# Third stage of a three-stage attention kernel: both runs of value products placed between head outputs and scores in TensorE's order

## The reference, cut to what matters

```python
def attn_layer(x, Wqkv, qs, ksc, Wo):                 # 16 heads of 64
    q, k, v = split(x @ Wqkv)                         # per head
    q = rotary(l2norm(q) * qs); k = rotary(l2norm(k) * ksc)
    sim = where(mask, -max, (q @ k.T) * 8.0)
    return (softmax(sim) @ v) @ Wo
for i in range(6):
    x = attn_layer(shift_tokens(x), ...) + x
    x = ffn_layer(shift_tokens(x), ...) + x           # layer norm, W1, a * gelu(gate), W2
```

## Time and profile before

| what | value |
|---|---|
| time, median of 3 runs | 3528.43 us (3526.76 to 3532.59) |
| time of the profiled execution | 3525.89 us |
| its span (first to last instruction) | 3524.1 us |
| TensorE busy | 3377.9 us, 96% of the span |
| VectorE / ScalarE / GpSimd busy | 2811.5 / 2792.7 / 2475.5 us |
| mean granted TensorE clock | 0.993 of full speed |

### The profile page before, as it was taken

The page is one execution under the profiler, slowest core; times in us unless marked ns, Lnnn a source line. Parts: engine busy times, 40 slices in busy tenths (PEclk is TensorE's granted clock), DMA queues, the critical chain, the costliest instruction groups (busy, mean ns, idle before and its releaser), DMA issues.

```text
span 3524.1 us, 120975 instructions
## 1 busy us (share of the span) xinstructions
PE 3377.9 (96%) x49605; PEld 2495.3 (71%) x49605; DVE 2811.5 (80%) x5297; ACT 2792.7 (79%) x5522; POOL 2475.5 (70%) x4812
## 2 busy tenths in 40 slices
PE   8989997999999999999999999999999999999997
PEld 5778774677777777777777777777777777777776
DVE  6834445888888888888888888888888888888885
ACT  5756664688888888888888888888888888888885
POOL 5622224777777777777777777777777777777774
PEclk9999998999999999999999999999999999999999
DMA  3000002444444444444444444444444444444441
GB/s 101 3 10 8 9 6 50 92 82 82 82 81 89 95 82 82 80 88 97 82 82 82 83 90 93 82 82 80 90 96 83 82 82 88 78 85 83 88 85 39
DMA packets 200382, 260.17 MB, mean 74 GB/s; under 512 B 123161, under 2 KB 145438, under 8 KB 199838
## 3 DMA queue, kind: packets, MB, share of 16 engines
q0 software_dynamic: 55296, 201.35, 30.4%
q1 hardware_dynamic: 143820, 50.88, 5.8%
q10 hardware_dynamic: 722, 0.21, 0.0%
HBM read 23.95 MB, written 2.10 MB: 7 GB/s over the span
## 4 chain that ended last, share of the span: by engine, by line
PE 78%; issue 2%; DVE 1%; POOL 1%; DMA 1%; ACT 0%; SPq 0%; POOLq 0%; DVEq 0%
PE bank L1032 18%; PE bank L1008 16%; PE bank L1083 10%; PE bank L1160 10%; PE bank L1128 7%; PE bank L1144 6%; PE bank L1103 5%; PE bank L1024 3%; PE bank L1098 2%; DVE R L1319 1%; DMA R<-R 1%; POOL R L1432 0%; POOL P L1444 0%; DVE ss L1332 0%; POOL P L1438 0%
## 5 line engine op out<-in xcount | busy, mean ns | idle before, releaser
L1319 DVE TENSOR_TENSOR R<-bank,tables 128x1024 f32<-128x1024 f32 x768 | 903.6, 1218 | 167.5 <-ACT sq L1219 127.4
L1032 PE MATMUL bank<-WA,xcT 128*128 128x512 f32 x1536 | 757.6, 596 | 1.8 <-ACT xcT L1194 1.8
L1008 PEld LDWEIGHTS bank<-ident,R 128*128 128x128 f32 x3072 | 371.6, 141 | 307.0 <-issue 299.9
L1444 POOL TENSOR_TENSOR P<-P,inv_sum 128x512 f32<-128x512 f32 x384 | 458.2, 1193 | 13.1 <-DVE inv_sum L1373 12.1
L1332 DVE TENSOR_REDUCE ss<-sq 128x16 f32<-128x1024 f32 x384 | 460.3, 1199 | 0.0
L1219 ACT ACTIVATE sq<-bank 128x512 f32<-128x512 f32 x768 | 438.2, 595 | 23.9 <-PE bank L1032 23.5
L1432 POOL TENSOR_TENSOR R<-R,rn 128x512 f32<-128x512 f32 x384 | 392.3, 1042 | 88.1 <-DMA R<-R 73.4
L1008 PE MATMUL bank<-ident,R 128*128 128x128 f32 x3072 | 429.8, 273 | 3.3 <-POOL R L1432 2.4
L1438 POOL TENSOR_TENSOR P<-P,rn 128x512 f32<-128x512 f32 x384 | 402.5, 1048 | 2.1 <-DVE P L1361 2.1
L1160 PE MATMUL bank<-WO,OT 128*128 128x128 f32 x3072 | 386.4, 279 | 1.7 <-ACT OT L1194 1.7
L1083 PE MATMUL bank<-WV,xcT 128*64 128x512 f32 x1536 | 376.0, 606 | 3.2 <-DVE R L1319 2.9
(11 more groups left out here) (154 smaller groups left out, 7082.5 us busy)
## 6 DMA issues: line engine op xcount, KB each, us to landing
R<-R POOLq DMA_DIRECT2D x384, 512.0 KB, 5.3
WA<-in_wqkv SPq DMA_DIRECT2D x24, 256.0 KB, 2.8
ystat<-Y SPq DMA_DIRECT2D x192, 32.0 KB
ystat<-Y SPq DMA_DIRECT2D x384, 15.8 KB
ys<-Y SPq DMA_DIRECT2D x192, 32.0 KB
ys<-Y SPq DMA_DIRECT2D x384, 15.8 KB
WV<-in_wqkv SPq DMA_DIRECT2D x6, 512.0 KB, 5.9
WO<-in_wo SPq DMA_DIRECT2D x6, 512.0 KB, 4.3
```

Of the source, the lines that this page charges most:

```text
L1008: return nc.tensor.transpose(dst, src, m.ident[:, :])
L1032: mm(b[QK_BANK[n, half]][:, :], m.xsT[:, t % 2, :], cols[:, half, :, :], start=True, stop=True)\
L1319: tt(both, src.unsqueeze(1).to_broadcast([128, 2, 16, 32]), tab.unsqueeze(2).to_broadcast([128, 2, 16, 32]), ALU.mult).then_inc(s.rotated. ...
L1444: tt(part, part, wide(m.inv_sum[:, t % 2, 8 * a:8 * a + 8]), ALU.mult).then_inc(s.normal.sem, 1)
```

## The change

On TensorE alone, the two calls of `values` move from behind `scores` to ahead of it. The orders of all other engines and the banks stay. For the first tiles one wait is added, since the copy of the turned queries out of bank 4 is no longer waited for by the scores ahead of the values.

```diff
                     else:
                         at_least(pe, s.o_copied.sem, s.o_copied.upto(0, t - 3))
+                        if t < 5:
+                            at_least(pe, s.q_copied.sem, s.q_copied.upto(1, t))
...
                 head_outputs(i - 4)
-                scores(i - 1)
                 values(i, 0)
                 values(i, 1)
+                scores(i - 1)
                 probs_turned(i - 3, 0)
```

## The result

The changed kernel takes 3547.49 us (median of 9 runs, 3543.39 to 3556.86) against 3530.24 us for the kernel before on the same chips: ratio 1.0048, 95% interval 1.0036 to 1.0060. It is slower by half a percent; 3549 us was forecast. The profiled execution has a span of 3545.4 us, 21.3 us more than before.

A forecast was written before the change was run, and what follows sets the result against it. TensorE was taken as the bound, unbroken at 14.66 us a turn except for 60 stops. Removing them (-84 us), adding waits (about 103) and remnants (2) gave +20: 3546 us profiled, 3549 median; 8 in 10 range 3533 to 3580.

The forecast's parts named there:

- The stops: 60 TensorE standstills at the scores, read as instruction packets coming too late; the change was to remove them, -84 us.
- the remnant behind the scores: Some late instruction packets at a new place, behind the last scores; 2 us of a possible 15 us was taken.
- 60 x 1.40 = 84 us: 60 turns with a standstill at the scores, each 1.40 us longer than a plain turn: the whole loss of 84 us.
- Some tenths: Claim about TensorE before the change: apart from some tenths, no turn waits for data.
- The wait: The moved value products wait for VectorE's first key rotation: 0.46 us idle plus 0.06 hand-over, 0.52 us paid in each turn.
- The last layer: Turns 168 to 191: an extra VectorE addition ahead of the key rotation makes the values' wait 0.80 us, turns 15.46 us.
- What is late behind the scores: Later scores delay VectorE's maximum to about 2026.4 from 2025.93; VectorE's idle times cover it, so it costs nothing.
- The sum: 160 turns of 15.18 us and 24 of 15.46 us against 2781.3 us: +18.5 us, about +20 with 2 us for remnants.
- The near cancellation: Two effects over the same turns, 84 and 103 us, nearly cancel, leaving the kernel 0.57% slower.
- the 84 and 103 us of the prediction: Over the turns of tiles 7 to 191: 84 us gained at the scores, 103 us lost to the values' wait.
- the first rival: The standstills at the scores all stay and only the values' wait counts: +102 us, 3631 us; chance 0.08 for all or most.

The follow-up runs named there:

- the corners above: Mean turns: kernel before 15.12 us; with only VectorE's sum of query squares moved behind the first key rotation 15.10; only TensorE's change 15.22; both 14.77.
- both edits: The changed kernel with VectorE's sum of the queries' squares moved behind the first key rotation: 3470.37 us, ratio 0.9858.

## Why the prediction was right

- **The stops are instruction supply.** Argued from counts then; now shown by three interventions. One instruction more a turn moves them by what it should, slow matmuls between the dense parts remove them with nothing else changed, and the real change removes all 60. The gain was sized at 84 us and the remnant behind the scores at 2 us; no remnant was found.
- **60 x 1.40 = 84 us matched the loss by luck.** The 1.40 us came from one turn. Averaged over the 60 turns with a stop, they are 1.23 us over a plain one, 74 us; the other 10 us lie in the 124 turns without one, half of them in the 11 turns in which a seam falls into the value products (up to 0.9 us each). "Some tenths" of waits for data were 3.7 us. The forecast held even so, since the 84 us also follow from the mean turn, 15.116 - 14.66, and the change removed both parts.
- **The wait costs 0.52 us a turn and is paid in each.** Measured 0.46 us idle and 0.05 us of hand-over, and turns of 15.17 us where 15.18 was worked out. The added copy shows that the loop has no slack: 0.30 us more of chain, 0.30 us more of turn.
- **The last layer.** 0.80 us was forecast from a single turn; it is 0.79 of idle time and the hand-over, and turns of 15.50 where I had 15.46. With the rarer longer ones their mean is 15.53. Up to tile 191 there are 23 such turns, not 24. This term was about 1 us short in sum.
- **What is late behind the scores.** The maximum starts 0.55 us later, counted from the turned input, and costs nothing, as said, since VectorE's idle times further on are still there.
- **The sum.** +19.9 us from tile 7 to 191 against +18.5 and 2 for remnants. The near cancellation was real: the corners above split it into 63 us gained and 83 lost. These are not the 84 and 103 us of the prediction, which count from turns of 14.66 us; with both edits the mean turn is 14.77, because other waits come up.
- **The Trainium skill** (Runtime: NRT & Kernel Launch, Instruction fetch mechanics) holds the crossing of a block to be mostly hidden. The block of 256 instructions agrees with the seams counted above. Hidden it is in most turns, yet 60 times in 184 it was not. The outcome by that page's rule is the first rival, which the prediction calls the second.

## What to carry to other kernels

When TensorE stands still with no releaser, look at what stands ahead of the stop: with many tiny matmuls in one stretch (here 132 in 2.4 us), count the instructions between two stops before looking for data. Slow matmuls between two dense stretches help only if their own wait stays covered, so before moving a step into such a gap, read when its latest input lands against its new start. And where a wait hangs, through other engines, on an earlier step of the same engine, it is paid in each turn; shorten that chain together with the reorder, as either alone gained nothing here.

## What the hardware showed that was not expected

The extra copy on VectorE took 0.215 to 1.134 us for the same 128x128 elements. VectorE and GpSimd in one turn of the changed kernel with the copy:

```profile
2566.09 1.05 POOL L1447 TENSOR_TENSOR P<-P,rn 128x512 f32<-128x512 f32 x1
2566.18 1.04 DVE L1391 COPY probe<-ident 128x128 f32<-128x128 f32 x1
```

It ends 0.08 us after GpSimd's multiplication. In the 78 turns in which no GpSimd instruction overlapped, the copy took 0.217 us on average; in the 97 in which one did, nearly always such a multiplication, 0.49 us; in the other 17 two or more did, 0.58 us. In all 96 turns in which the copy took over 0.25 us, it ended 0.081 to 0.086 us after a GpSimd instruction. The Trainium skill (SBUF — State Buffer, SBUF: two separate sides) describes a port pair shared by the two engines that the first to start keeps for its whole instruction. The trace agrees. That is why this copy cost 0.30 us a turn and not the 0.2 expected: before the last layer, turns without overlap average 15.32 us and those with one 15.60, where the kernel without the copy has 15.18.

A seam costs more than its idle row shows: a turn with a stop is on average 1.23 us over a plain one, against 0.91 us of idle time.
